# Graph layer with a norm on one Trainium2 core: a quarter of one tile's rows is fetched by single-row DMAs from SyncE

## The reference

```python
h = feat[src]                                   # E x 64
for r, w_r in enumerate(weight):                # 16 relations, 64 x 64 each
    m = m + where(etypes == r, 1, 0)[:, None] * (h @ w_r)
out = segment_sum(m, dst, num_segments=3125)    # N x 64
x = layernorm(x + out, axis=-1)                 # no scale, no shift
```

## Time and profile before

| | before |
|---|---|
| time, median of 3 runs | 820.51 us (819.25 to 821.03) |
| time of the profiled execution | 818.77 us |
| its span | 817.0 us |
| mean granted TensorE clock in it | 0.975 |
| PE, DVE, ACT, POOL busy | 681.3, 600.2, 584.4, 594.1 us |
| gathers of POOL | 620 |
| DMA traffic over the span | 71 GB/s |

### The profile page before, as it was taken

The page is one execution under the profiler, slowest core; times in us unless marked ns, Lnnn a source line. Parts: engine busy times, 40 slices in busy tenths (PEclk is TensorE's granted clock), DMA queues, the critical chain, the costliest instruction groups (busy, mean ns, idle before and its releaser), DMA issues.

```text
span 817.0 us, 24513 instructions
## 1 busy us (share of the span) xinstructions
PE 681.3 (83%) x8136; PEld 640.5 (78%) x8137; DVE 600.2 (73%) x2221; ACT 584.4 (72%) x1325; POOL 594.1 (73%) x634
## 2 busy tenths in 40 slices
PE   0688888888888988889888889888898888898896
PEld 0687788788877977878878878878788788788785
DVE  5988667786776786676875867777768768777756
ACT  5776767776777777768777777677687767776753
POOL 3777777777777777777777777777777777777770
PEclk9999999999999999999999999999999999999997
DMA  8222222222233222222222222222222222222121
GB/s 210 67 72 73 70 65 71 66 69 71 62 73 71 63 71 70 64 71 65 69 71 61 74 71 62 73 71 64 71 64 71 71 61 74 71 61 74 51 52 48
DMA packets 31416, 57.75 MB, mean 71 GB/s; under 512 B 12360, under 2 KB 20546, under 8 KB 31402
## 3 DMA queue, kind: packets, MB, share of 16 engines
q0 software_dynamic: 19840, 40.67, 19.7%
q1 hardware_dynamic: 11254, 16.10, 7.3%
q10 hardware_dynamic: 308, 0.80, 0.5%
HBM read 55.12 MB, written 2.40 MB: 70 GB/s over the span
## 4 chain that ended last, share of the span: by engine, by line
POOL 65%; issue 26%; DVE 4%; PE 2%; DMA 1%; ACT 1%; POOLq 1%; ACTq 0%; DVEq 0%
POOL rows L295 65%; DVE pick L468 1%; DMA x_sb<-in_x 1%; PE own L692 1%; PE own L831 0%; POOLq L197 0%; ACT pick L384 0%; ACT away L378 0%; DMA rows<-x_parts,gidx 0%; DVE onehot L534 0%; DVE x_sb L606 0%; DVE src_f L521 0%; DVE tmin L494 0%; DVE xp L489 0%; DVE tmax L495 0%
## 5 line engine op out<-in xcount | busy, mean ns | idle before, releaser
L295 POOL DMA_INDIRECT rows<-x_parts,gidx x620 | 587.8, 948 | 200.8 <-issue 188.1
L692 PE MATMUL own<-xp,pick 125*128 125x192 bf16 x4650 | 410.4, 252 | 77.1 <-issue 75.4
L692 PEld LDWEIGHTS own<-xp,pick 125*128 125x128 bf16 x4650 | 395.5, 100 | 87.7 <-issue 85.8
L468 DVE TENSOR_SCALAR pick<-src_h,node 125x384 bf16<-125x384 f16 x1240 | 401.8, 400 | 0.0
L534 DVE TENSOR_SCALAR onehot<-ramp,krel 128x112 bf16<-128x112 bf16 x806 | 149.4, 260 | 49.7 <-issue 49.7
L378 ACT ACTIVATE away<-src_h,node_neg 125x384 bf16<-125x384 f16 x310 | 169.6, 613 | 0.1
L384 ACT ACTIVATE pick<-away,one 125x384 bf16<-125x384 bf16 x310 | 163.1, 611 | 0.0
L730 PE MATMUL agg<-onehot,rows 128*128 128x112 bf16 x2418 | 138.6, 213 | 28.5 <-DMA rows<-x_parts,gidx 25.4
L392 ACT ACTIVATE rows<-own 128x192 bf16<-128x192 f32 x186 | 61.6, 332 | 138.4 <-PE own L692 131.7
L730 PEld LDWEIGHTS agg<-onehot,rows 128*128 128x128 bf16 x2418 | 120.8, 98 | 47.9 <-issue 47.8
L552 DVE TENSOR_TENSOR outT<-outT,rel 64x32 f32 x124 | 22.3, 180 | 149.7 <-PE rel L742 141.1
(11 more groups left out here) (62 smaller groups left out, 73.2 us busy)
## 6 DMA issues: line engine op xcount, KB each, us to landing
src_b<-in_src SPq DMA_DIRECT2D x62, 192.0 KB
rows<-x_parts,gidx POOLq DMA_INDIRECT x620
x_parts<-xp SPq DMA_DIRECT2D x1, 728.0 KB
x_parts<-xp SPq DMA_DIRECT2D x1, 672.0 KB
out<-x_sb SPq DMA_DIRECT2D x2, 224.0 KB
x_sb<-in_x ACTq DMA_DIRECT2D x1, 364.0 KB
x_sb<-in_x ACTq DMA_DIRECT2D x1, 336.0 KB
src_i<-in_src SPq DMA_DIRECT2D x1, 312.0 KB
```

The costliest lines, as they stand in the source:

```text
L295: pool.indirect_dma_start(rows[:, u, j, :], None, x_parts, bass.IndirectOffsetOnAxis(ap=gidx[:, u, j:j + 1], axis=0)).then_inc(rows_in[u] ...
L468: v.tensor_scalar(pick[u][:, b, :], src_h[u][:, :, 0:CUTW[u]], node[:, b:b + 1], None, ALU.is_equal).then_inc(pick_ready[u], 1)
L692: return nc.tensor.matmul(own[h][:, 0:SPLIT * D], pick[u][:, b, h * P:(h + 1) * P], xp[:, b, 0:SPLIT, :].rearrange("p s d -> p (s d)"), st ...
```

## The change

For tile 9 of each half (STILE), the rows of edges 96 to 127 are no longer gathered by POOL. SP loads their 32 source indices into a tile of one partition (`load_single`), reads all 32 into registers by one TENSOR_LOAD, and issues 32 DMAs of one row each, 512 bytes, whose address in `x_parts` comes from a register (`single_fetch`). They count on a semaphore of their own, `single_rows[u]`, for which PE waits ahead of tile 9. POOL's gather of that tile has 96 rows in place of 128; the number of its gathers stays ten a half. SP's `spread_sources` is now called one turn ahead, in the order that `turn` shows, and SP waits for the stored table and then runs its first turn ahead of the loop.

```diff
--- before.py
+++ after.py
@@ -67,6 +67,9 @@
     GQ = 48
     PARTS = ((0, NQ), (NQ, NP))
     RQ = R // 2
+    SINGLE = 32
+    STILE = 9
+    SQ = P - SINGLE
 
     x_parts = nc.dram_tensor("x_parts", [N, RP * D], bf16, kind="Internal").ap()
 
@@ -101,6 +104,7 @@
         far = sb("far", [G, GT])
         shift = sb("shift", [G, GT])
         par = sb("par", [G, PW], i32)
+        single = [sb(f"single{u}", [1, SINGLE], i32) for u in range(2)]
         par_row = sb("par_row", [1, G * PW], i32)
         any_far = sb("any_far", [1, 1], i32)
 
@@ -167,6 +171,7 @@
         par_set, par_in, any_set = sem("par_set"), sem("par_in"), sem("any_set")
         xT_done, xT_taken = sem("xT_done"), sem("xT_taken")
         gidx_ready, rows_in, late_in = sem2("gidx_ready"), sem2("rows_in"), sem2("late_in")
+        single_in, single_rows = sem2("single_in"), sem2("single_rows")
         src_b_in, src_h_ready, pick_ready = sem2("src_b_in"), sem2("src_h_ready"), sem2("pick_ready")
         away_ready, act_pick_ready = sem("away_ready"), sem2("act_pick_ready")
         own_done, own_rows = sem2("own_done"), sem2("own_rows")
@@ -247,15 +252,44 @@
                 for p0, p1 in PARTS:
                     sp.dma_start(pv[p0:p1, b0:b1, :], xp[p0:p1, b0:b1, :, :].rearrange("p b s d -> p b (s d)")).then_inc(parts_out, 16)
 
-            def turn(i):
-                spread_sources(i, 0)
-                spread_sources(i, 1)
+            def load_single(i, u):
+
+                a = src[bass.ds(i * (2 * ROW) + (u * ROW + STILE * P + SQ), SINGLE)]
+                sp.dma_start(single[u][:, :], a.rearrange("(o e) -> o e", o=1)).then_inc(single_in[u], 16)
+
+            def single_fetch(i, u):
+
+                sp.wait_ge(single_in[u], (i + 1) * 16)
+                sp.nop(nofuse=True)
+                at = nc.values_load_multi_w_load_instructions(
+                    single[u][0:1, 0:SINGLE], engines=[mybir.EngineType.SP], min_val=0, max_val=N - 1,
+                    skip_runtime_bounds_check_because="a node index of the edge list")[1]
+                if not is_first(i):
+                    sp.wait_ge(agg_ready[u], i)
+                sp.nop(nofuse=True)
+                for k in range(SINGLE):
+                    sp.dma_start(rows[SQ + k:SQ + k + 1, u, STILE, :], x_parts[bass.ds(at[k], 1), :]).then_inc(single_rows[u], 16)
+
+            def turn(i, more=True):
+                if more:
+                    spread_sources(i + 1, 0)
+                single_fetch(i, 0)
+                if more:
+                    load_single(i + 1, 0)
+                    spread_sources(i + 1, 1)
+                single_fetch(i, 1)
+                if more:
+                    load_single(i + 1, 1)
+            load_single(0, 0)
+            load_single(0, 1)
             for q in range(2):
                 sp.dma_start(w_pair[q * D:(q + 1) * D, :, :],
                              weight.rearrange("(q two) k d -> two k q d", two=2)[q]).then_inc(w_in, 16)
             sp.wait_ge(par_set, 3)
             sp.dma_start(par_row[:, :], par[:, :]).then_inc(par_in, 16)
-            group_loop(sp, turn, first=1)
+            sp.wait_ge(parts_out, 64)
+            group_loop(sp, turn, last=LAST)
+            turn(LAST, more=False)
             with go_general(sp):
                 sp.dma_start(g_w[:, :, :], weight.rearrange("r k d -> k r d")).then_inc(g_w_in, 16)
             for n in range(YT):
@@ -292,9 +326,10 @@
                 pool.wait_ge(gidx_ready[u], i + 1)
                 pool.nop(nofuse=True)
                 for j in range(OWN[u], GT):
+                    q = SQ if j == STILE else P
                     pool.indirect_dma_start(
-                        rows[:, u, j, :], None, x_parts,
-                        bass.IndirectOffsetOnAxis(ap=gidx[:, u, j:j + 1], axis=0)).then_inc(rows_in[u] if j < LATE else late_in[u], 16)
+                        rows[0:q, u, j, :], None, x_parts,
+                        bass.IndirectOffsetOnAxis(ap=gidx[0:q, u, j:j + 1], axis=0)).then_inc(rows_in[u] if j < LATE else late_in[u], 16)
 
             def turn(i):
                 fetch(i, 0)
@@ -724,6 +759,8 @@
                 for j in range(GT):
                     if j == OWN[u]:
                         pe.wait_ge(rows_in[u], (i + 1) * (16 * (LATE - OWN[u])))
+                    if j == STILE:
+                        pe.wait_ge(single_rows[u], (i + 1) * (16 * SINGLE))
                     if j == LATE:
                         pe.wait_ge(late_in[u], (i + 1) * (16 * (GT - LATE)))
                     for s in range(SPLIT):
```

## The result

The changed kernel takes 1074.94 us (median of 4 runs, 1074.50 to 1075.26), the kernel before, run beside it, 820.58 (4 runs, 819.25 to 821.03): a ratio of 1.310, with a 95% interval of 1.308 to 1.313. The forecast was 1040, with a range of 920 to 1180 and slower at 0.94.

A forecast was written before the change was run, and what follows sets the result against it. POOL's gathers, 12.5 us a half, bound the kernel before; SP, at 16.1, would bound after. 62 halves make 998, less 1.8; plus 21.3 start, 2.5 landing, 17.9 end and 1.8: 1040 us, range 920 to 1180.

The forecast's parts named there:

- The bound: SP's serial work, 16.1 us a half against 12.4 on POOL, sets the time, so POOL's saving is worth nothing.
- The rows: SP's 32 single rows a half: 0.13 register work, 0.23 issue, 0.04 gap, 0.40 each, 12.8 us.
- TENSOR_LOAD with `spread_sources` and the waits: On SP per half: loading 32 values 2.17 us, spreading sources 0.50, two fulfilled waits and an arithmetic instruction 0.12.
- `load_single` and the loop's turn: On SP per half: one more one-row DMA 0.40 us; the loop's move, addition and branch 0.12.
- POOL's side: One gather of ten shrinks to 96 rows, saving 0 to 0.24 us a half, middle 0.12, 7 us over 62 halves.
- The rival with SP hidden: SP's half fits under POOL's 12.5 us, so POOL still bounds: 804 to 819 us, middle 811; chance 0.06.
- nothing gained: Case with SP hidden where POOL's 96-row gather costs like one of 128; chance 0.02.
- Waits and order: SP's wait for `agg_ready` and its sources spread a turn ahead cause no stall; waits are late by nothing.
- The end: After SP's last row: 2.5 us for a landing, 17.7 for the end, 0.2 for one more tile.
- Issue independent of size: Rival: each DMA issue in SP's loop costs 333 ns whatever it moves, a half 19.4 us, 1245 us; chance 0.10.
- The queue backs up: Rival: SP's single-row DMAs wait for their queue, 1.2 us a row, a half 41.7, about 2600 us; chance 0.02.
- DMA engines: SP's queue moves 1984 more packets of 512 bytes, some 1.3% of the engines' time, costed at nothing.

The follow-up runs named there:

- fixed_address_b: Changed kernel with its 32 single-row DMAs a half at fixed addresses, without TENSOR_LOAD and register arithmetic: 819.03 us against 820.38 for the kernel before.
- order_alone: Changed kernel without single-row DMAs, index loads and PE's wait for them, POOL gathering 128 rows again, SP's new order kept: 1340.78 us against 1341.12 for the kernel before.
- lighter_pe: Changed kernel with 13 of PE's 25 `own` products in each loop turn: 1581.38 us against 1315.82 for the kernel before, ratio 1.202.
- fixed_address: Changed kernel with single-row DMAs at fixed addresses, no TENSOR_LOAD or register arithmetic, in a slow set: 1413.68 us against 1315.82 for the kernel before.

## Why the prediction was right, step by step

- **The bound.** "SP becomes the bound; POOL's saving is worth nothing then": the chain, the waits and `fixed_address_b` show it. SP's half is 16.67 us where 16.1 was predicted, and 62 x 0.57 = 35 us are the whole difference between 1040 and 1075 (SP's first TENSOR_LOAD stands at 22.2 and not at 21.3, and the end is 0.5 shorter; these two nearly cancel).
- **The rows**: 12.8 predicted; 508.24 to 521.45 and 525.12 to 538.47 give 13.28. The issue was 0.228 for 0.23. The sum of register instructions and gaps was the mis-sized term: 0.413 - 0.228 = 0.185 against 0.17 (0.13 + 0.04). The two register instructions are 66 ns of the 185, which leaves 119 for the gaps between the three instructions of a row, 40 ns each. It is the largest miss, 0.48 a half, 30 us in all.
- **TENSOR_LOAD with `spread_sources` and the waits**: 2.17 + 0.50 + 0.12 = 2.79 predicted; 505.54 to 508.24 and 522.33 to 525.12 give 2.75. Within it the load was 2.03, for 2.13 by the slope from PE's and DVE's rows, and the issue of `spread_sources` 361 ns for 333: it cost 28 ns more here than in the kernel before. In `order_alone` it is 333 again, so it comes with the single rows and not with the order; why wasn't sought.
- **`load_single` and the loop's turn**: 0.40 + 0.12 = 0.52 predicted; (0.88 + 0.41) / 2 = 0.65 measured. A turn-round is 0.65 - 0.18 = 0.47 us (the gap behind `load_single` at one end of the turn, 521.68 to 522.33, against the one inside it, 505.36 to 505.54), twice the 0.24 summed from the earlier trace rows.
- **POOL's side.** "Between such ends I take the middle, 0.12": this step failed. A 96-row gather saves 0.034 us (0.91 for 0.945), near the lower end, 0, of its range of 0 to 0.24, so the best case of this change is not 804 or 811 but about 819, which `fixed_address_b` gives. The total doesn't show the error, since SP hid it: that part of the forecast was right by luck. The rival with SP hidden would have come out as 819, its "nothing gained".
- **Waits and order**: late by nothing, as forecast. SP has no wait in its loop, POOL took 258.0 us of waits for `agg`, PE waits for `rows<-x_parts` at tile 9.
- **The end**: one row's landing was about 1.0 us (1053.3 + 0.23 to PE's next weight load for `agg` at 1054.56), for 2.5 taken from a gather; the rest 18.8 for 17.9. Together 19.9 against 20.4.
- **Issue independent of size** is out: 228 ns for one row beside 361 for 128 in the same loop. The Trainium skill, DMA: Bandwidth & Descriptors, section Why a DMA increments its semaphore by 16 and not by 1, has 512 cycles for a plain DMA, the estimate of 427 ns of the prediction: neither of the two issue times agrees with it. A row's whole step, 413 ns, comes close, but only 228 of that is the DMA. With a fixed address the step is 294 ns, though the issue itself is then 252 and not 228.
- **The queue backs up** is out: no issue of the 1984 took over 294 ns.
- **DMA engines.** "1984 more" packets was a wrong count, without effect: SP's queue moved 15346 packets for the 11254 of the earlier trace rows, 4092 more, two for each of the 1984 rows and 62 index loads. In `fixed_address_b` its share rose from 7.3% to 8.1%.

The Trainium skill, on that page, in its section Rules for kernel authors, says that spreading DMAs over the issuing engines only saves sequencer issue time. These runs didn't spread DMAs over engines, but they show what such time can be worth: in `fixed_address_b` the transfers cost nothing, and the serial time of SP's sequencer (issue, address arithmetic, loads of addresses) made the kernel after 254 us slower.

## What to carry to other kernels

Cost a DMA with an address from a register at the sequencer, per instruction (here 0.41 us a row, and 2.03 us to load 32 addresses), and compare the sum of one period with the bound's period: an idle engine is only free as long as its serial work fits. Before moving rows away from an indirect gather, measure what a smaller gather costs: here a quarter of the rows was 2 to 4% of its time, so whole gathers would have to go, not parts of them (that was not tried). To tell a DMA's address work from its transfer, give the same DMAs a fixed address: one changed line separated them.

## What was not expected of the hardware

- A TENSOR_LOAD on SP took 487 ns for 1 value, 638 for 2, 1137 for 16, 1582 for 24 and 2030 for 32: 36 ns a value from 2 to 16 and 56 from 16 on, no plateau. The Trainium skill gives about 600 ns as its floor (DMA: Bandwidth & Descriptors, Latency and other measured facts); that is near the 638 of two values on SP, above the 487 of one, and under a third of the 2030 of 32.
- An indirect gather on POOL costs 944 ns for 128 rows and 911 to 922 for 96: 2 to 4% less for a quarter fewer rows. Fewer than 96 were not tried alone.
- In three sets the same kernel before took 1316 to 1341 us for 820. The trace of `order_alone`, as slow as it, has a granted clock of 0.73 for 0.975, and 267.2 us of gaps ahead of PE's `own` products for 75.4, about 0.7 us from one start to the next; a further 23% of its chain is put down to no engine of this core. In the same sets the kernels in which SP issues single rows were 6 to 8% slower still (`lighter_pe` 20%), with PE's gaps at 515 to 535 us, about twice the 240 to 328 of the kernels without single rows (not in `lighter_pe`), and with single instructions of SP of 1.4 us (at most 0.3 at L271 in the kernel after). In the set at 820 the same kernel as `fixed_address` was no slower at all. The cause wasn't found.
